# The last feed-forward layer's routing: experts ranked on the router's logits, softmax weights made on other engines, list keys in fewer steps

## The chip, the cores and the metric

One Trainium2 chip (trn2), one core. The metric is the device time of one execution of the whole program, in microseconds, as the median of several runs. The engines are named TensorE (PE, with its weight loads as PEld), VectorE (DVE), ScalarE (ACT), GpSimd (POOL) and SyncE (SP, which here only issues DMAs). L2147 is line 2147 of the kernel before.

## The reference

A network of four layers on x of 8 x 128 tokens with 256 features. Each layer adds an attention part and a feed-forward part, both on the layer-normalised x. Only the last feed-forward part is touched, a mixture of 64 experts with 8 for each token and room for 128 tokens in each expert:

```python
x = hidden_states.reshape(-1, H)                 # 1024 tokens, H = 256
logits = x @ router_weight.T                     # 64 experts
probs = softmax(logits, axis=-1)
topw, topi = top_k(probs, 8)
topw = topw / sum(topw, axis=-1, keepdims=True)
flat_e = topi.reshape(-1)
oh = one_hot(flat_e, E)
pos = take_along_axis(cumsum(oh, axis=0), flat_e[:, None], axis=1)[:, 0] - 1
xe = zeros((E, 128, H)).at[flat_e, pos].set(repeat(x, 8), mode='drop')
g, u = split(einsum('ech,ehf->ecf', xe, gate_up_proj), 2)   # 96 each
ye = einsum('eci,eih->ech', silu(g) * u, down_proj)
y_flat = where((pos < 128)[:, None], ye[flat_e, minimum(pos, 127)], 0)
y = sum(y_flat.reshape(-1, 8, H) * topw[..., None], axis=1)
```

A token whose place in an expert is 128 or later is dropped there.

## The kernel before, in words

The eight parts (four attentions, four feed-forwards) run one after the other, each a block with a program for every engine, ordered by semaphores. The last one is `moe_l3`. Tokens lie as 8 tiles (B) of 128 partitions, so that most of its routing steps are one instruction over 128 x (8 x 64) elements. `Chain` counts VectorE's steps: `link` issues a step and waits until it is done, `add` issues it alone, and `wait` waits for all steps added.

**Ahead of the experts**, in the order of the data:

- TensorE makes the logits in PSUM, `lg` (L2044).
- VectorE takes the row maximum (L2137) and subtracts it (L2138); ScalarE takes the exponential (L2112); VectorE sums (L2140), inverts (L2141) and multiplies (L2142). The probabilities are `ex`.
- VectorE takes the eight largest of each row (MAX8, L2144, 8 instructions), replaces them by -1 in a copy, `left` (MATCH_REPLACE with a value load, L2147, 8 pairs), and makes the 0/1 mask from it (L2149). `masked` is signalled.
- TensorE makes `pos` from the mask: how many earlier tokens chose the expert (L2050, 36 matmuls, `ranked`). Beside it VectorE makes the weights: sum of the eight best (L2150), inverse (L2151), product (L2152), product with the mask (L2155).
- VectorE counts along the row (scan, L2157), makes a number for each chosen slot, falling with the token (L2158), masks it (L2160), and sets it to zero where `pos` is 64 or more (L2162, the keys of list half one) and 128 or more (L2163); the difference is half two (L2164, `keyed`). L2165 zeroes the weights of dropped tokens (`weighed`), in `cw`.
- TensorE transposes the keys to expert x token (L2055, two groups of four). ScalarE copies group one (L2116) and VectorE group two (L2167) to SBUF.
- VectorE draws the 64 largest keys of each row, eight at a time: MAX8 (L2171) and MATCH_REPLACE (L2174) over 1024 elements, eight rounds. The list is turned (L2060) and made into slot numbers and token numbers (L2177 to L2180, `indexed`). Empty places point to a row of zeros.

**The token table** `xw` in HBM holds for each token its 256 features and 64 weights, and 128 zero rows. ScalarE's queue writes it with three DMAs: the features (L2108), the zero rows (L2110), and the weight columns when `weighed` (L2114). Each adds 16 to `table_in`.

**The experts' loop**: GpSimd gathers 128 rows for an expert with an indirect DMA (L2021), six experts ahead; the first needs `indexed` and all of `table_in`. TensorE turns them (L2068), multiplies (L2078), turns h (L2086), multiplies (L2093). ScalarE does Silu (L2124) and scales the result with the gathered weight (L2130). VectorE copies and multiplies (L2186, L2198, L2192). GpSimd scatters the 128 result rows to `rows` in HBM (L2026). SyncE prefetches the experts' weights in 16 loads of four experts (L1996), six of which start at once. At the end the eight rows of each token are read back and added on VectorE (L2210, L2211).

Of the kernel before, what the change touches and what calls it, by code (L numbers as in the profile page):

```python
# [12 lines left out]
ALU = mybir.AluOpType  # L13
ACT = mybir.ActivationFunctionType
AX = mybir.AxisListType.X

P = 128
D = 256
KD = D // P
B = 8  # L20
T = B * P
LN_EPS = 1e-5
HALF = 512
# [1908 lines left out]
def moe_l3(pg, pre, xw, rows):  # L1932

    nc, E, K, CAP, F = pg.nc, 64, 8, 128, 96
    GROUP, LOADS, AHEAD, NY = 4, 6, 6, 4
    ROW = D + E
    W = 2 * 2 * F + D
    names = ("const", "ones_in", "steps", "logits", "shifted", "exped", "masked", "ranked", "keyed", "weighed", "turned", "key_kept",
             "listed", "list_turned", "indexed", "table_in", "zero_in", "x_turned", "x_kept", "gu_done", "silued", "h_made", "h_turned",
             "h_kept", "y_done", "y_kept", "summed", "stored")  # L1940
    s = {m: pg.sem(f"l3m_{m}") for m in names}
# [4 lines left out]
    with ExitStack() as st:  # L1946
        def sb(m, shape, dt=F32):
            return st.enter_context(nc.sbuf_tensor(f"l3m_{m}", shape, dt))
        def wide_of(at, n):
            return pg.l2_wx[:].rearrange("p k n -> p (k n)")[:, at:at + n].rearrange("p (b e) -> p b e", b=B)  # L1950
        rw, = pre.tiles
        ex = wide_of(0, B * E)
# [3 lines left out]
        mt = wide_of(1536, B * E)  # L1956
        tmp = wide_of(2048, B * E)
        best = sb("best", [P, B, 8])
        small = sb("small", [P, 4, B])
# [47 lines left out]
        def _(pool):  # L2007
# [20 lines left out]

            pool.wait_ge(s["indexed"], 1)
# [77 lines left out]
        def _(act):  # L2107
# [4 lines left out]
            nc.scalar.activation(ex[:], ex[:], ACT.Exp).then_inc(s["exped"], 1)  # L2112
            act.wait_ge(s["weighed"], 1)
            act.dma_start(rows_of(xw)[:, :, D:ROW], cw[:]).then_inc(s["table_in"], 16)  # L2114
            act.wait_ge(s["turned"], 1)
            nc.scalar.activation(kb[:, 0, 0:HALF], key_ps[0][:], ACT.Copy).then_inc(s["key_kept"], 1)  # L2116
# [16 lines left out]
        def _(dve):  # L2133
# [3 lines left out]
            ch.link(v.tensor_reduce(small[:, 0, :], lg, AX, ALU.max))  # L2137
            v.tensor_tensor(ex[:], lg, small[:, 0, :].unsqueeze(2).to_broadcast(wide), ALU.subtract).then_inc(s["shifted"], 1)  # L2138
            dve.wait_ge(s["exped"], 1)
            ch.link(v.tensor_reduce(small[:, 1, :], ex[:], AX, ALU.add))  # L2140
            ch.link(v.reciprocal(small[:, 2, :], small[:, 1, :]))  # L2141
            ch.link(v.tensor_tensor(ex[:], ex[:], small[:, 2, :].unsqueeze(2).to_broadcast(wide), ALU.mult))  # L2142
            for t in range(B):
                ch.add(v.max(best[:, t, :], ex[:, t, :]))  # L2144
            ch.wait()
            for t in range(B):
                ch.add(v.match_replace(left[:, t, :], best[:, t, :], ex[:, t, :], -1.0))  # L2147
            ch.wait()
            v.tensor_scalar(mask[:], left[:], 0.0, None, ALU.is_lt).then_inc(s["masked"], 1)  # L2149
            ch.link(v.tensor_reduce(small[:, 0, :], best[:], AX, ALU.add))  # L2150
            ch.link(v.reciprocal(small[:, 3, :], small[:, 0, :]))  # L2151
            ch.link(v.tensor_tensor(ex[:], ex[:], small[:, 3, :].unsqueeze(2).to_broadcast(wide), ALU.mult))  # L2152
            dve.wait_ge(s["masked"], 1)
            dve.wait_ge(s["const"], 3)
            ch.add(v.tensor_tensor(ex[:], ex[:], mask[:], ALU.mult))  # L2155
            flat = mask[:].rearrange("p b e -> p (b e)")
            ch.link(v.tensor_tensor_scan(count[:], flat, flat, 0.0, ALU.add, ALU.max))  # L2157
            ch.link(v.scalar_tensor_tensor(out=mt[:], in0=count[:].rearrange("p (b e) -> p b e", b=B), scalar=-1.0,  # L2158
                                           in1=token[:].unsqueeze(2).to_broadcast(wide), op0=ALU.mult, op1=ALU.add))
            ch.link(v.tensor_tensor(mt[:], mt[:], mask[:], ALU.mult))  # L2160
            dve.wait_ge(s["ranked"], 1)
            ch.add(v.scalar_tensor_tensor(out=key[:, :, 0:E], in0=pos, scalar=float(CAP // 2), in1=mt[:], op0=ALU.is_lt, op1=ALU.mult))  # L2162
            ch.link(v.scalar_tensor_tensor(out=tmp[:], in0=pos, scalar=float(CAP), in1=mt[:], op0=ALU.is_lt, op1=ALU.mult))  # L2163
            v.tensor_tensor(key[:, :, E:2 * E], tmp[:], key[:, :, 0:E], ALU.subtract).then_inc(s["keyed"], 1)  # L2164
            v.scalar_tensor_tensor(out=cw[:], in0=pos, scalar=float(CAP), in1=ex[:], op0=ALU.is_lt, op1=ALU.mult).then_inc(s["weighed"], 1)  # L2165
# [201 lines left out]
```

## Time and profile before

| | us |
|---|---|
| median of 3 runs | 1994.09 |
| lowest and highest | 1990.58 to 1999.31 |
| the profiled execution | 1990.2 |
| its span | 1988.5 |
| TensorE busy (share of the span) | 1623.6 (82%) |
| VectorE busy | 1174.5 (59%) |
| ScalarE busy | 807.2 (41%) |
| GpSimd busy | 616.7 (31%) |

The span runs from the first to the last instruction of one profiled execution; the device time of that execution is a little longer. The granted TensorE clock is a share of its full speed of 2.4 GHz. A chain of work goes back from the last instruction, at each step to what released it. In a row of the timeline the brackets tell how long the engine sat idle before the instruction and what ended that.

### The profile page before, as it was taken

The page shows a single profiled execution, that of the slowest core. Times are in us where ns is not written, and L with a number is a line of the kernel's source. Part 1 is how long each engine was busy: PE and PEld are TensorE (multiplying, and loading weights), DVE is VectorE, ACT ScalarE, POOL GpSimd, SP SyncE. Part 2 cuts the span into 40 slices and gives each one's busy share as a digit, 9 for nine tenths or more (in the row PEclk, how much of TensorE's full clock was granted, in tenths as well). Part 3 has the DMA queues.
Part 4 walks back from the last instruction along what each step waited for, and adds up shares of the span by engine and source line. Part 5 has one row for each costly group of instructions (what it writes and reads, how often), then busy time and mean ns, then how long its engine had stood idle before and what let it go on. Part 6 is the DMA issues. An engine that isn't in the chain of part 4 may idle for free. (4 is left out here: it accounts for less than half of the span.)

```text
span 1988.5 us, 25186 instructions
## 1 busy us (share of the span) xinstructions
PE 1623.6 (82%) x8472; PEld 1004.2 (51%) x8472; DVE 1174.5 (59%) x2662; ACT 807.2 (41%) x1848; POOL 616.7 (31%) x979
## 2 busy tenths in 40 slices
PE   6688878999786899995388998998699989637772
PEld 5323234556454455553166666666555555435552
DVE  5799972223554642426789999999822255552325
ACT  3888773111322211112377777777621112312221
POOL 0022211000200197900455555655210000036662
PEclk9755558999687899997699999999899998767886
DMA  2288872110501213111100000000101100435635
GB/s 72 52 161 162 157 149 62 40 40 16 170 1 66 99 57 124 55 49 38 48 1 1 1 1 1 1 1 1 41 22 38 40 23 1 162 104 202 208 127 223
DMA packets 174224, 140.12 MB, mean 70 GB/s; under 512 B 141793, under 2 KB 154721, under 8 KB 170386
## 3 DMA queue, kind: packets, MB, share of 16 engines
q1 hardware_dynamic: 165314, 114.89, 20.6%
q0 software_dynamic: 6416, 22.03, 3.3%
q10 hardware_dynamic: 2368, 1.61, 0.3%
q8 instruction: 69, 1.13, 0.2%
q14 instruction: 57, 0.47, 0.1%
HBM read 85.43 MB, written 19.50 MB: 53 GB/s over the span
## 5 line engine op out<-in xcount | busy, mean ns | idle before, releaser
L1417 PE MATMUL l2x_pr<-l_w,l2x_xq 128*128 128x512 bf16 x576 | 142.4, 385 | 40.9 <-ACT credits L42 40.4
L350 PE MATMUL l1e_gu<-x_normT,l1e_w 128*128 128x512 f32 x384 | 170.8, 599 | 0.0
L1875 ACT ACTIVATE l0m_pf<-l0m_s,l0m_bias,l0x_sq 128x1024 int16<-128x1024 f32 x128 | 154.1, 1204 | 38.9 <-POOL l0m_bias L1807 38.9
L1901 DVE TENSOR_REDUCE l0m_mx<-l0m_s 128x1 f32<-128x1024 f32 x128 | 156.0, 1220 | 21.6 <-PE l0m_s L1817 20.1
L1817 PE MATMUL l0m_s<-l0x_kT,l0x_qT 48*128 48x512 bf16 x256 | 126.2, 620 | 35.8 <-ACT l0m_pf L1875 31.7
L350 PE MATMUL l0e_gu<-x_normT,l0e_w 128*128 128x512 f32 x272 | 121.5, 601 | 0.0
L1807 POOL TENSOR_SCALAR l0m_bias<-l0m_mx,l0x_nsq 128x1 f32<-128x1 f32 x128 | 46.7, 365 | 225.0 <-DVE l0m_mx L1901 223.6
L350 PEld LDWEIGHTS l1e_gu<-x_normT,l1e_w 128*128 128x128 f32 x384 | 73.8, 193 | 83.8 <-issue 82.7
L350 PE MATMUL l2e_gu<-x_normT,l2e_w 128*128 128x512 f32 x256 | 115.0, 604 | 0.0
L1546 DVE TENSOR_SCALAR l2x_raw<-l2x_raw,l2x_mv,l2x_rs 128x128 f32<-128x128 f32 x384 | 111.3, 352 | 3.5 <-POOL l2x_rs L1396 3.3
L1417 PEld LDWEIGHTS l2x_pr<-l_w,l2x_xq 128*128 128x128 bf16 x576 | 57.0, 99 | 97.3 <-ACT credits L42 40.8
L426 DVE TENSOR_TENSOR l1e_h<-l1e_sil,l1e_gu 128x512 f32<-128x512 f32 x40 | 27.5, 688 | 133.1 <-ACT l1e_sil L402 133.1
L1400 POOL TENSOR_TENSOR x_norm<-x_norm,l2x_rsm 128x512 f32<-128x512 f32 x64 | 74.9, 1171 | 97.2 <-DVE l2x_rsm L1552 97.2
L1536 DVE BATCH_NORM_STATS2 l2x_bn<-l2x_raw 128x6 f32<-128x128 f32 x384 | 82.5, 279 | 34.2 <-ACT l2x_raw L1485 34.1
L402 ACT ACTIVATE l1e_sil<-l1e_gu 128x512 f32<-128x512 f32 x48 | 28.6, 596 | 178.6 <-PE l1e_gu L350 178.6
L1437 PE MATMUL l2x_tr<-ident,l2x_raw 128*128 128x128 f32 x384 | 60.9, 281 | 44.7 <-DVE l2x_raw L1546 44.0
L1490 ACT ACTIVATE x_norm<-l2x_s,l2x_mx 128x128 f32<-128x128 f32 x256 | 90.3, 372 | 2.4 <-DVE l2x_mx L1541 2.4
L357 PE MATMUL l1e_y<-l1e_w,l1e_h 128*128 128x256 f32 x384 | 86.1, 379 | 0.0
L426 DVE TENSOR_TENSOR l0e_h<-l0e_sil,l0e_gu 128x512 f32<-128x512 f32 x28 | 19.3, 688 | 112.4 <-ACT l0e_sil L402 112.4
L1396 POOL TENSOR_TENSOR l2x_rs<-l2x_rs,l2x_half 128x8 f32<-128x8 f32 x48 | 82.7, 1723 | 3.8
L350 PEld LDWEIGHTS l0e_gu<-x_normT,l0e_w 128*128 128x128 f32 x272 | 52.4, 193 | 60.0 <-issue 59.3
L357 PEld LDWEIGHTS l1e_y<-l1e_w,l1e_h 128*128 128x128 f32 x384 | 73.0, 190 | 18.5 <-issue 9.6
(522 smaller groups left out, 3633.3 us busy)
## 6 DMA issues: line engine op xcount, KB each, us to landing
l3m_w<-in_l_moe SPq DMA_DIRECT2D x16, 1280.0 KB
l1e_w<-in_l_ffn SPq DMA_DIRECT2D x24, 384.0 KB, 3.1
l_rows<-zero_row SPq DMA_DIRECT2D x8, 1024.0 KB, 11.1
l_w<-l_rows SPq DMA_DIRECT2D x8, 1024.0 KB, 11.9
l0e_w<-in_l_ffn SPq DMA_DIRECT2D x17, 384.0 KB, 3.1
l2e_w<-in_l_ffn SPq DMA_DIRECT2D x16, 384.0 KB, 3.1
ctx_tok<-l_route SPq DMA_DIRECT2D x8, 512.0 KB
l2q_wps<-in_l_wp SPq DMA_DIRECT2D x16, 256.0 KB, 2.7
```

The source lines that it names most:

```text
L350: last = nc.tensor.matmul(gu[half][:, m, :], w[:, c % SW, (2 * k + m) * P:(2 * k + m + 1) * P], pg.xnT[:, k, cols(n)], start=(k == 0), sto ...
L357: last = nc.tensor.matmul(y[:, t, :], h[:, c % SH, t * P:(t + 1) * P], w[:, c % SW, WG:CHUNK], start=(c == 0 and t % 2 == 0), stop=False, ...
L1396: g.tensor_tensor(rs[:, 1, two, :], var, half[:, 0], ALU.pow).then_inc(s["rstd"], 1)
L1400: nc.gpsimd.tensor_tensor(p[:, a % 2], p[:, a % 2], rsm[:, a % 2].unsqueeze(2).to_broadcast([P, U, P]), ALU.mult).then_inc(s["p_normed"], 1)
L1417: last = nc.tensor.matmul(flat(pr[t % 2][:]), src[:, k, tokens], pg.l2_w3[:, part, k, at:at + W], start=(k == 0 and part == 0), stop=(k == ...
L1437: last = nc.tensor.transpose(tr[:, j, :], raw[:, u, j, :], pg.ident[:])
L1490: last = nc.scalar.activation(p[:, a % 2, j, :], s_ps[a % 2][:, j, :], ACT.Exp, bias=mx[:, a % 2, j:j + 1], accum_out=sm[:, a % 2, j:j + 1])
L1536: last = nc.vector.bn_stats(bn[:, t, j, :], raw[:, t, j, :])
L1546: last = nc.vector.tensor_scalar(raw[:, u, j, :], raw[:, u, j, :], mv[:, u, j, 0:1], rs[:, 1, u, j:j + 1], ALU.subtract, ALU.mult)
L1817: last = nc.tensor.matmul(s_ps[n % 3][:, g * HALF:(g + 1) * HALF], qT[:, h, b * P:(b + 1) * P], kT[:, h, g * HALF:(g + 1) * HALF], start=T ...
L1875: nc.scalar.activation(pf[:, n % 4, :], s_ps[n % 3][:], ACT.Exp, scale=sq[:, b, h:h + 1], bias=bias[:, n % 4:n % 4 + 1], accum_out=sm[:, b ...
L1901: nc.vector.tensor_reduce(mx[:, n % 4:n % 4 + 1], s_ps[n % 3][:], AX, ALU.max).then_inc(s["maxed"], 1)
```

## The change

The rank is taken on the logits, which softmax leaves in the same order. VectorE draws the eight largest logits (`best`), makes the negated maximum from the first, replaces the eight in a copy and makes the mask. ScalarE makes, beside it, the exponentials of the eight best with their sum (8 instructions with an accumulator output) and, once the mask is done, the exponentials of all 64 logits with the negated maximum as bias (8 instructions). VectorE inverts the sums of eight after the keys, and GpSimd multiplies, which gives `cw` with no mask: weights of experts that a token did not choose are never gathered. ScalarE copies the first half of the turned keys before it waits for `weighed` and issues the weight columns' DMA. The keys of half one are no longer cut at place 64 nor those of half two at place 128, since the lists hold 64 each and take the earliest tokens first; half two keeps the places from 64 on.

```diff
@@ -1934,8 +1934,9 @@
+    GONE = -3.0e38
@@ -1953,10 +1954,10 @@
         mask = sb("mask", [P, B, E], BF16)
-        mt = wide_of(1536, B * E)
         tmp = wide_of(2048, B * E)
         best = sb("best", [P, B, 8])
-        small = sb("small", [P, 4, B])
+        top = sb("top", [P, B, 8])
+        small = sb("small", [P, 3, B])
@@ -2026,6 +2027,9 @@
                 g.indirect_dma_start(out=rows, out_offset=bass.IndirectOffsetOnAxis(ap=slot[:, e:e + 1], axis=0),
                                      in_=ye[:, e % NY, :], in_offset=None).then_inc(put[e % NY], 16)
 
+            pool.wait_ge(s["exped"], B)
+            pool.wait_ge(s["top_inverse"], 1)
+            g.tensor_tensor(cw[:], ex[:], small[:, 2, :].unsqueeze(2).to_broadcast([P, B, E]), ALU.mult).then_inc(s["weighed"], 1)
             pool.wait_ge(s["indexed"], 1)
             pool.wait_ge(s["table_in"], 48)
             for e in range(AHEAD):
@@ -2109,11 +2113,16 @@
             act.wait_ge(s["zero_in"], 1)
             act.dma_start(xw[T:T + P, :], zero[:]).then_inc(s["table_in"], 16)
             act.wait_ge(s["shifted"], 1)
-            nc.scalar.activation(ex[:], ex[:], ACT.Exp).then_inc(s["exped"], 1)
+            for n in range(B):
+                nc.scalar.activation(top[:, n, :], best[:, n, :], ACT.Exp, bias=small[:, 0, n:n + 1], accum_out=small[:, 1, n:n + 1])\
+                    .then_inc(s["summed_top"], 1)
+            act.wait_ge(s["masked"], 1)
+            for n in range(B):
+                nc.scalar.activation(ex[:, n, :], lg[:, n, :], ACT.Exp, bias=small[:, 0, n:n + 1]).then_inc(s["exped"], 1)
+            act.wait_ge(s["turned"], 1)
+            nc.scalar.activation(kb[:, 0, 0:HALF], key_ps[0][:], ACT.Copy).then_inc(s["key_kept"], 1)
             act.wait_ge(s["weighed"], 1)
             act.dma_start(rows_of(xw)[:, :, D:ROW], cw[:]).then_inc(s["table_in"], 16)
-            act.wait_ge(s["turned"], 1)
-            nc.scalar.activation(kb[:, 0, 0:HALF], key_ps[0][:], ACT.Copy).then_inc(s["key_kept"], 1)
 
             for i in range(E + 2):
                 if 1 <= i <= E:
@@ -2134,35 +2143,26 @@
             v, ch = nc.vector, Chain(dve, s["steps"])
             wide = [P, B, E]
             dve.wait_ge(s["logits"], 1)
-            ch.link(v.tensor_reduce(small[:, 0, :], lg, AX, ALU.max))
-            v.tensor_tensor(ex[:], lg, small[:, 0, :].unsqueeze(2).to_broadcast(wide), ALU.subtract).then_inc(s["shifted"], 1)
-            dve.wait_ge(s["exped"], 1)
-            ch.link(v.tensor_reduce(small[:, 1, :], ex[:], AX, ALU.add))
-            ch.link(v.reciprocal(small[:, 2, :], small[:, 1, :]))
-            ch.link(v.tensor_tensor(ex[:], ex[:], small[:, 2, :].unsqueeze(2).to_broadcast(wide), ALU.mult))
-            for t in range(B):
-                ch.add(v.max(best[:, t, :], ex[:, t, :]))
+            for n in range(B):
+                ch.add(v.max(best[:, n, :], lg[:, n, :]))
             ch.wait()
-            for t in range(B):
-                ch.add(v.match_replace(left[:, t, :], best[:, t, :], ex[:, t, :], -1.0))
+            v.tensor_scalar(small[:, 0, :], best[:, :, 0], -1.0, None, ALU.mult).then_inc(s["shifted"], 1)
+            for n in range(B):
+                ch.add(v.match_replace(left[:, n, :], best[:, n, :], lg[:, n, :], GONE))
             ch.wait()
-            v.tensor_scalar(mask[:], left[:], 0.0, None, ALU.is_lt).then_inc(s["masked"], 1)
-            ch.link(v.tensor_reduce(small[:, 0, :], best[:], AX, ALU.add))
-            ch.link(v.reciprocal(small[:, 3, :], small[:, 0, :]))
-            ch.link(v.tensor_tensor(ex[:], ex[:], small[:, 3, :].unsqueeze(2).to_broadcast(wide), ALU.mult))
+            v.tensor_scalar(mask[:], left[:], GONE, None, ALU.is_le).then_inc(s["masked"], 1)
             dve.wait_ge(s["masked"], 1)
             dve.wait_ge(s["const"], 3)
-            ch.add(v.tensor_tensor(ex[:], ex[:], mask[:], ALU.mult))
             flat = mask[:].rearrange("p b e -> p (b e)")
             ch.link(v.tensor_tensor_scan(count[:], flat, flat, 0.0, ALU.add, ALU.max))
-            ch.link(v.scalar_tensor_tensor(out=mt[:], in0=count[:].rearrange("p (b e) -> p b e", b=B), scalar=-1.0,
+            ch.link(v.scalar_tensor_tensor(out=tmp[:], in0=count[:].rearrange("p (b e) -> p b e", b=B), scalar=-1.0,
                                            in1=token[:].unsqueeze(2).to_broadcast(wide), op0=ALU.mult, op1=ALU.add))
-            ch.link(v.tensor_tensor(mt[:], mt[:], mask[:], ALU.mult))
+            ch.link(v.tensor_tensor(key[:, :, 0:E], tmp[:], mask[:], ALU.mult))
             dve.wait_ge(s["ranked"], 1)
-            ch.add(v.scalar_tensor_tensor(out=key[:, :, 0:E], in0=pos, scalar=float(CAP // 2), in1=mt[:], op0=ALU.is_lt, op1=ALU.mult))
-            ch.link(v.scalar_tensor_tensor(out=tmp[:], in0=pos, scalar=float(CAP), in1=mt[:], op0=ALU.is_lt, op1=ALU.mult))
-            v.tensor_tensor(key[:, :, E:2 * E], tmp[:], key[:, :, 0:E], ALU.subtract).then_inc(s["keyed"], 1)
-            v.scalar_tensor_tensor(out=cw[:], in0=pos, scalar=float(CAP), in1=ex[:], op0=ALU.is_lt, op1=ALU.mult).then_inc(s["weighed"], 1)
+            v.scalar_tensor_tensor(out=key[:, :, E:2 * E], in0=pos, scalar=float(CAP // 2), in1=key[:, :, 0:E], op0=ALU.is_ge, op1=ALU.mult)\
+                .then_inc(s["keyed"], 1)
+            dve.wait_ge(s["summed_top"], B)
+            v.reciprocal(small[:, 2, :], small[:, 1, :]).then_inc(s["top_inverse"], 1)
             dve.wait_ge(s["turned"], 2)
             v.tensor_copy(kb[:, 0, HALF:T], key_ps[1][:]).then_inc(s["key_kept"], 1)
             dve.wait_ge(s["key_kept"], 2)
```

## Rows read from the trace of the kernel before

**Rows 1.** Stretches: ranking and keys, lists, experts' loop.
```profile
core 0: us, PE busy (x) PEld busy (x) DVE busy (x) ACT busy (x) POOL busy (x), PEclk, DMA share, GB/s
1726.60:1742.10 15.50, 4.00 (x44) 3.52 (x44) 12.97 (x41) 1.39 (x3) 0.00 (x0) 0.50 1.01 416
1742.10:1763.80 21.70, 0.52 (x5) 0.29 (x4) 20.36 (x27) 1.12 (x1) 0.00 (x0) 0.50 0.10 28
1763.80:1956.70 192.90, 139.63 (x576) 106.55 (x576) 57.18 (x192) 45.79 (x128) 124.83 (x128) 0.78 0.50 165
```

**Rows 2.** Chain that ended last, in order of time: start us, us, what.
```profile
1726.61 0.70 DVE l3m_small L2137
...
1728.06 0.64 ACT l_wx L2112
...
1730.41 1.13 DVE l3m_best L2144 x8
...
1731.56 1.66 DVE l_wx L2147 x9
1733.21 0.02 issue
1733.23 0.43 DVE l3m_mask L2149
...
1739.43 0.70 DVE l_wx L2164
```

**Rows 3.** Timeline: start us, us, engine, line; idle before and its releaser last.
```profile
1735.40 1.22 DVE L2157 TENSOR_TENSOR_SCAN l_wx<-l3m_mask 128x512 f32<-128x512 bf16 x1
...
1735.64 0.24 PE L2050 MATMUL l3m_ps<-l3m_mask,l3m_before 128*128 128x64 bf16 x1
...
1740.75 0.38 ACTq L2114 DMA_DIRECT2D l_xw<-l_wx  x1
1741.33 0.60 ACT L2116 ACTIVATE l_w<-l3m_ps 128x512 f32<-128x512 f32 x1 [12.64 <-PE l3m_ps L2055]
...
1742.18 0.69 DVE L2167 COPY l_w<-l3m_ps 128x512 f32<-128x512 f32 x1 [1.46 <-PE l3m_ps L2055]
...
1764.04 1.15 POOL L2021 DMA_INDIRECT l3m_xg<-l_xw,l3m_idx  x1 [43.48 <-DVE l3m_idx L2180]
```

**Rows 4.** Groups of instructions, shapes apart: busy us, mean ns | idle before, releasers.
```profile
L2164 DVE TENSOR_TENSOR l_wx<-l_wx 128x512 f32<-128x512 f32 x1 | 0.7, 693 | 0.0
...
L2137 DVE TENSOR_REDUCE l3m_small<-l3m_ps 128x8 f32<-128x512 f32 x1 | 0.7, 692 | 7.4 <-PE l3m_ps L2044 7.4
...
L2140 DVE TENSOR_REDUCE l3m_small<-l_wx 128x8 f32<-128x512 f32 x1 | 0.7, 686 | 0.7 <-ACT l_wx L2112 0.7
...
L2141 DVE RECIPROCAL l3m_small<-l3m_small 128x8 f32<-128x8 f32 x1 | 0.2, 203 | 0.0
...
L2124 ACT ACTIVATE l3m_sil<-l3m_ps 128x96 f32<-128x96 f32 x64 | 16.1, 251 | 132.0 <-PE l3m_ps L2078 71.0 <-remote 44.8 <-issue 16.0
```

**Rows 5.** Timeline of ScalarE in an earlier layer, exponentials with an accumulator.
```profile
1002.48 0.37 ACT L1490 ACTIVATE x_norm<-l2x_s,l2x_mx 128x128 f32<-128x128 f32 x1 [0.95 <-DVE l2x_mx L1541]
1002.75 0.19 ACT L1490 ACTIVATION_READ_ACCUMULATOR x_norm<-l2x_s,l2x_mx 128x1 f32 x1
1002.84 0.36 ACT L1490 ACTIVATE x_norm<-l2x_s,l2x_mx 128x128 f32<-128x128 f32 x1
```

**Rows 6.** One line's instructions on GpSimd: duration ns min/median/max, first and last start.
```profile
L1400 POOL TENSOR_TENSOR x_norm<-x_norm,l2x_rsm x64: 1034/1129/1378, 1002.6 to 1421.5; 128x512 f32<-128x512 f32 x64
```

**Rows 7.** DMA issues of the last layer: KB each, median us to landing.
```profile
l_xw<-l_wx ACTq DMA_DIRECT2D x1, 256.0 KB, 5.3
l_xw<-l3m_zero ACTq DMA_DIRECT2D x1, 160.0 KB, 24.0
```

**Rows 8.** Two stretches of the experts' loop, columns as in rows 1.
```profile
1800.00:1810.00 10.00, 9.18 (x33) 7.87 (x34) 3.21 (x11) 2.07 (x6) 5.89 (x6) 0.57 0.43 139
1870.00:1880.00 10.00, 4.95 (x25) 3.38 (x25) 2.22 (x8) 1.49 (x5) 7.13 (x8) 1.00 0.67 234
```

More of the change, by code:

```diff
@@ L1936, in moe_l3 @@
     ROW = D + E
+    GONE = -3.0e38
     W = 2 * 2 * F + D
-    names = ("const", "ones_in", "steps", "logits", "shifted", "exped", "masked", "ranked", "keyed", "weighed", "turned", "key_kept",
+    names = ("const", "ones_in", "steps", "logits", "shifted", "summed_top", "top_inverse", "exped", "masked", "ranked", "keyed", "weighed", "turned", "key_kept",
              "listed", "list_turned", "indexed", "table_in", "zero_in", "x_turned", "x_kept", "gu_done", "silued", "h_made", "h_turned",
```

## The prediction, made blind

> **What bounds the kernel now.** The profiled execution took 1990.2 us, with a span of 1988.5 us and 1.7 us around it. The median of the three timed runs is 1994.09 us, 3.9 us above the profiled one. The runs themselves lie between 1990.58 and 1999.31 us. I make the sum on the span and then take it off the median.
>
> I read three views, in this order. First, the stretches of the last layer [rows 1]. The ranking and key stretch lasts 15.5 us. VectorE is busy for 12.97 of it and TensorE for 4.00. Behind it come 21.7 us in which VectorE alone makes the lists (20.36 busy), and then 192.9 us of expert loop, where no engine is full: TensorE 139.6 busy, GpSimd 124.8. So a step saved on VectorE ahead of the loop moves everything behind it. Second, the chain of work that ended last, in order of time [rows 2]. From 1726.61 to 1740.13 it runs through every VectorE step of the ranking, with one 0.64 us ScalarE step between. Nothing else is on it: the whole softmax stands in line ahead of the ranking. Third, the single instructions with their starts [rows 3], for what the other engines have ready, and when.
>
> **The path to the keys, before.** It starts at 1726.61 and ends with the subtraction at 1739.43 + 0.70 = 1740.13, so 13.52 us [rows 2].
>
> **The path to the keys, after.** A link, a step that waits for the one before it, costs 0.02 us, as at 1733.21 [rows 2].
> - Eight MAX8 on the logits 1.13, link 0.02, negation of 128x8 taken at 0.20 as the reciprocal of the same shape [rows 4], eight MATCH_REPLACE with their value loads 1.66, link 0.02, mask 0.43 [rows 2]. The sum is 3.46 us, so the mask is done at 1730.07 instead of 1733.66.
> - Wait on the mask, taken a little over a link, 0.03, scan 1.22 at its full length [rows 3], link 0.02, two 512-element steps with a link each, 2 x 0.71, and one last 512-element step 0.69 [rows 4]. The sum is 3.38 us, so the keys are done at 1733.45.
> - Sum 6.84 against 13.52: **6.68 us less**, of which 3.59 ahead of the mask (two reductions, subtraction, exponential, reciprocal, multiplication, less the new negation) and 3.09 behind it (second normalisation, mask product, one of the two position tests, the subtraction).
>
> **Logits read where they lie.** MAX8 and MATCH_REPLACE now read PSUM, which no row shows for them. The nearest pair is a reduction of 512 elements, 692 ns from PSUM and 686 ns from SBUF [rows 4]. I take 6 ns for each of 16 instructions, 0.1 us, which I leave in the range. The row's difference, nothing against 0.1, gives both ends. The Trainium skill (VectorE: DVE Perf Modes, "The TRN2 errata") gives VectorE 120 fixed cycles for a PSUM source against 58 for an SBUF one, at 0.96 GHz. By the page, as an estimate, the 16 instructions would cost 1.0 us more, and the gain would be 5.7. The reduction's two rows speak against it.
>
> **The position counts.** The chain must not wait for TensorE. Its last count matmul ended at 1735.64 + 0.24 = 1735.88, 2.22 us after the mask [rows 3]. After the change that is 1732.29, and VectorE asks for it at 1732.76. The cover is 0.47 us. If the matmuls take longer than that, the excess is lost one for one. Their clock cannot fall: it is at its lower level, 0.50 or 1.2 GHz, through both stretches, with 4.00 of 15.5 us busy [rows 1].
>
> **ScalarE's new work.** It may start at 1728.0. Eight exponentials with an accumulator: the nearest rows are pairs of an ACTIVATE of 128x128 and an accumulator read, which start 0.36 us apart [rows 5]. So 2.9 us is the upper end, and 2.1 the lower, with 120 elements less at 0.84 ns, which the 512-wide copy's 0.60 us and the 96-wide Silu's 0.25 us give (0.35 us for 416 elements) [rows 3, 4]. Eight exponentials of 128x64: between 0.25 (the 96-wide Silu, no bias operand) [rows 4] and 0.36 each [rows 5], 2.0 to 2.9 us. ScalarE is free between 1732.1 and 1733.8. What hides it is the position part of the chain. ScalarE's next duty is the copy of the first half of the transposed keys. It began 1.20 us after the keys [rows 2, 3], now 1734.65, so 0.85 to 2.55 us of cover are left. A further 0.9 us stands behind it, because VectorE's own half ended later (1742.87 against 1741.93) [rows 3]. If that cover goes, VectorE's first list round waits for the copy.
>
> **GpSimd's multiplication.** It waits for those exponentials and for the reciprocal behind the keys (1733.45 + 0.20). Two-input products of 128x512 on GpSimd take 1034 to 1378 ns [rows 6], so it ends between 1734.7 and 1735.2. Queued behind it on GpSimd are only the gathers, which wait for the indices until 1757 anyway. It reads SBUF while VectorE waits for the transposes. VectorE loses a product of 512 elements (0.69) and gains the reciprocal (0.20), both behind the keys and ahead of a wait for TensorE that lasted 1.46 us [rows 3], so they cost nothing.
>
> **The weight column's DMA.** It is the same DMA, but now queued behind ScalarE's copy: issue at about 1735.3 instead of 1740.75 [rows 3]. It moves no other step back, since the Silu table load behind it is needed only in the loop. Its landing took 5.3 us, that of the zero block, issued into the weight prefetch, 24.0 us [rows 7]. That gives 1740.6 to 1759.3. The gathers want it at 1757.4. I take the lower end plus some wait, about 1746: the DMA share falls from 1.01 to 0.10 at 1742.1 [rows 1], so nothing is left to queue behind. The upper end would cost 1.9 us.
>
> **The lists and the loop.** List rounds, transposes, indices, gathers and the experts' loop are the same instructions, moved up by 6.7 us. The first gather should start at 1764.04 - 6.68 = 1757.36. By the span: 1988.5 - 6.7 = 1981.8, by the profiled execution 1990.2 - 6.7 = 1983.5, by the median **1994.1 - 6.7 = 1987.4 us**.
>
> **The rivals.**
> - *ScalarE becomes the bound (chance 0.10).* If ScalarE ended 3.8 us later than its upper bound (0.85 + 0.9 of cover, then 2 us on the path), or the weight column landed at its upper end (1.9 us), some 2 us come back: 1989.4 us. For it: 24 ScalarE instructions stand where one did. Against it: 0.85 us of cover at the upper bounds.
> - *The loop runs better in its new place (chance 0.15).* The loop is 29 times as long as the gain. GpSimd is busy for 124.8 of 192.9 us, and in two stretches of ten microseconds the granted clock is 0.57 and 1.00 [rows 8], means over its two levels (0.50 is 1.2 GHz, 1.00 is 2.4 GHz). If a sixth of the 30 us that TensorE's half-clock time costs went away (139.6 us at 0.78 is 109 at full clock), that is 5 us: 1982.4 us. Against it: nothing inside the loop is changed, so it is chance.
> - *The loop falls badly (chance 0.05), slower than before.* The place is the experts' loop, and the mechanism the granted clock. 139.6 us of TensorE work at a mean of 0.78 [rows 1] become 146.3 at 0.744, which eats the whole gain, and 156.3 at 0.697, which is the point where the kernel is 0.5% slower, if all of it lies on the path. At 0.73 the cost is 9.6 us and the time 1997.0. For it: the timed runs of one kernel already span 8.7 us. Against it: a mean over 193 us has to move. The Trainium skill (TensorE: Matmul & The Clock Gate, Part 1) says that the number of slow matmuls at the start of the same kernel changes from run to run; one trace cannot show that here. By that rule the loop's time could drift either way, and no step of the change steers it.
>
> **How the numbers follow.** The forecast, 6.7 us less, has 0.70. A measurement of this kernel can tell some 0.5% from no change, which is 10 us; the forecast is 0.34%, so it counts as within 0.5%. Faster by more than that needs a time under 1984.1: the second rival, and a little of the forecast's scatter, 0.19 together. Slower needs over 2004: part of the third rival, 0.03. The rest, 0.78, is within 0.5%. The range: downwards the scatter of the median (1994.09 - 1990.58 = 3.5) and half of the second rival's extra, which gives 1981; upwards 5.2 for the scatter (1999.31 - 1994.09) and 2.4 for the first rival, 1995.
>
> **What would show it.** Right: MAX8 at the start of the chain, mask about 3.5 us after the logits, last key step about 6.8 us after them; ScalarE done with its sixteen exponentials before its copy of the keys; the first gather near 1757.4; a loop of 193 us, give or take 5. Wrong: idle time of the first list round or of VectorE's key copy released by ScalarE, idle time of the last key step released by the counts, MAX8 of 64 elements clearly over 0.14 us apart, the first gather released by the weight column's DMA, or a loop whose length moved by more than the gain.

## The result, and the profile after

| | before | after |
|---|---|---|
| median of 20 runs, us | 1995.14 | 1988.17 |
| lowest and highest | 1990.58 to 2001.98 | 1983.2 to 1994.02 |
| profiled execution, span | 1990.2, 1988.5 | 1987.75, 1986.0 |

The ratio of after to before is 0.9961, 95% interval 0.9951 to 0.9971: 7.8 us less, between 5.8 and 9.8. The medians lie 7.0 us apart. The interval lies clear of 1, so the kernel is faster, but by less than the 0.5% that the forecast set as its line; it counts as within 0.5%, as forecast.

The stretches of the changed kernel's last layer, cut at the same events as before (busy us and count of each engine, granted clock, DMA share, GB/s). They answer to [rows 1]:

```profile
core 0: us, PE busy (x) PEld busy (x) DVE busy (x) ACT busy (x) POOL busy (x), PEclk, DMA share, GB/s
1730.38:1739.22 8.84, 4.01 (x44) 3.52 (x44) 6.75 (x31) 4.74 (x26) 1.05 (x1) 0.50 1.04 429
1739.22:1760.90 21.68, 0.52 (x5) 0.29 (x4) 20.36 (x27) 1.12 (x1) 0.00 (x0) 0.50 0.41 150
1760.90:1954.32 193.42, 135.88 (x576) 103.83 (x576) 56.98 (x192) 45.22 (x128) 124.84 (x128) 0.81 0.49 165
```

From the logits to the start of VectorE's copy of the turned keys are 8.84 us where it was 15.5. The lists (21.68 against 21.70) and the loop (193.4 against 192.9) keep their lengths. ScalarE is busy for 4.74 us instead of 1.39, GpSimd for 1.05 instead of nothing.

The chain that ended last (start us, us, what), which answers to [rows 2]:

```profile
1730.39 1.16 DVE l3m_best L2147 x8
...
1731.58 0.17 DVE l3m_small L2149
1731.75 1.60 DVE l_wx L2151 x8
...
1733.37 0.44 DVE l3m_mask L2153
...
1733.83 1.24 DVE l_wx L2157
...
1736.55 0.70 DVE l_wx L2162
...
1737.29 1.99 PE l3m_ps L2059 x8
...
1739.30 0.70 DVE l_w L2167
```

It starts at 1730.39 and the last key step ends at 1737.25: **6.86 us** against 13.52. No ScalarE and no GpSimd piece stands in it. Ahead of the mask's end lie 3.42 us (the prediction had 3.46), behind it 3.44 (3.38).

Single instructions of the other engines, from the timeline (idle time and its releaser in brackets), which answer to [rows 3]:

```profile
1734.08 1.70 ACT L2121 ACTIVATE l_wx<-l3m_ps,l3m_small 128x64 f32<-128x64 f32 x8
...
1735.78 0.24 PE L2054 MATMUL l3m_ps<-l3m_mask,l3m_before 128*128 128x64 bf16 x1
...
1737.50 1.05 POOL L2032 TENSOR_TENSOR l_wx<-l_wx,l3m_small 128x512 f32<-128x512 f32 x1 [13.15 <-DVE l3m_small L2165]
1738.45 0.60 ACT L2123 ACTIVATE l_w<-l3m_ps 128x512 f32<-128x512 f32 x1 [2.68 <-PE l3m_ps L2059]
1738.58 0.38 ACTq L2125 DMA_DIRECT2D l_xw<-l_wx  x1
...
1761.16 1.15 POOL L2022 DMA_INDIRECT l3m_xg<-l_xw,l3m_idx  x1 [22.61 <-DVE l3m_idx L2180]
```

The last count matmul ends at 1736.02, and the key step that needs it starts at 1736.55. ScalarE's sixteen exponentials end at 1735.78, and it sits idle for 2.68 us before its copy of the keys. The first gather is released by the indices.

All profiled executions can be laid side by side at the end of the logits. The table holds milestones read from their timelines, in us, those marked + counted from that end; "loop" runs from the first gather's start to the last scatter's end. The kernels of one letter B, C or D ran on one chip, with before beside them; A are the two of the result.

| kernel | logits end at | first transpose | first list round | first gather | loop | group |
|---|---|---|---|---|---|---|
| before | 1726.57 | +13.60 | +16.34 | +37.47 | 193.6 | A |
| after | 1730.36 | +6.93 | +9.67 | +30.80 | 194.1 | A |
| a_rank_only | 1726.45 | +8.26 | +10.99 | +32.12 | 179.5 | B |
| b_keys_only | 1729.66 | +12.27 | +15.00 | +36.13 | 175.1 | B |
| e_dve9 | 1728.09 | +13.45 | +16.18 | +37.31 | 177.6 | B |
| e_dve28 | 1728.17 | +27.28 | +30.01 | +51.14 | 178.1 | B |
| c_pool8 | 1728.61 | +6.94 | +9.67 | +30.80 | 180.5 | C |
| c_pool24 | 1731.00 | +6.94 | +9.67 | +38.59 | 177.3 | C |
| d_act_order | 1728.18 | +6.93 | +9.66 | +30.79 | 180.6 | C |
| before_again | 1728.56 | +13.59 | +16.33 | +37.46 | 194.3 | D |
| after_again | 1728.42 | +6.93 | +9.66 | +30.78 | 194.1 | D |
| f_act16 | 1727.60 | +6.93 | +11.48 | +32.60 | 193.8 | D |
| h_halves | 1733.71 | +4.54 | +7.27 | +28.40 | 194.4 | D |

In the two profiled executions of the first two lines the first gather is 6.67 us closer to the logits. The spans differ by only 2.5 us, since the parts ahead of the last one, where nothing was changed, happened to take 3.79 us longer (1730.36 - 1726.57) and the loop 0.5 us, less 0.1 behind it: 3.79 - 6.67 + 0.5 - 0.1 = -2.5. In the second pair of the same two kernels, before_again and after_again, the logits end within 0.14 us of each other and the loops are 0.2 us apart, and there the spans differ by 7.1 us (1991.2 and 1984.1).

### The profile page after: what moved, and what is told of

Its sections match the earlier page's. It is cut to its first block and busy times, and to the rows that moved or that the text cites. A ratio compares the mean times of both kernels' runs of the same rounds, so it can differ in the third digit from the quotient of the medians.

```text
span 1986.0 us, 25201 instructions
## 1 busy us (share of the span) xinstructions
PE 1622.9 (82%) x8472; PEld 1004.9 (51%) x8472; DVE 1170.6 (59%) x2652; ACT 809.9 (41%) x1871; POOL 616.7 (31%) x980
## 3 DMA queue, kind: packets, MB, share of 16 engines
q8 instruction: 69, 1.13, 0.2%
## 5 line engine op out<-in xcount | busy, mean ns | idle before, releaser
L1901 DVE TENSOR_REDUCE l0m_mx<-l0m_s 128x1 f32<-128x1024 f32 x128 | 155.8, 1219 | 21.8 <-PE l0m_s L1817 20.3
L402 ACT ACTIVATE l1e_sil<-l1e_gu 128x512 f32<-128x512 f32 x48 | 28.6, 596 | 179.4 <-PE l1e_gu L350 179.4
L426 DVE TENSOR_TENSOR l0e_h<-l0e_sil,l0e_gu 128x512 f32<-128x512 f32 x28 | 19.3, 688 | 110.7 <-ACT l0e_sil L402 110.7
L357 PEld LDWEIGHTS l1e_y<-l1e_w,l1e_h 128*128 128x128 f32 x384 | 72.9, 190 | 19.4 <-issue 9.1
```

The costliest lines, as they stand in the source:

```text
L357: last = nc.tensor.matmul(y[:, t, :], h[:, c % SH, t * P:(t + 1) * P], w[:, c % SW, WG:CHUNK], start=(c == 0 and t % 2 == 0), stop=False, ...
L1901: nc.vector.tensor_reduce(mx[:, n % 4:n % 4 + 1], s_ps[n % 3][:], AX, ALU.max).then_inc(s["maxed"], 1)
```

## The experiments

**Half of the change each.** First the ranking on the logits with the weights beside it, and the keys as before:

```diff
 after, with the keys of before:
...
-            v.scalar_tensor_tensor(out=key[:, :, E:2 * E], in0=pos, scalar=float(CAP // 2), in1=key[:, :, 0:E], op0=ALU.is_ge, op1=ALU.mult)\
-                .then_inc(s["keyed"], 1)
+            ch.add(v.scalar_tensor_tensor(out=key[:, :, 0:E], in0=pos, scalar=float(CAP // 2), in1=mt[:], op0=ALU.is_lt, op1=ALU.mult))
+            ch.link(v.scalar_tensor_tensor(out=tmp[:], in0=pos, scalar=float(CAP), in1=mt[:], op0=ALU.is_lt, op1=ALU.mult))
+            v.tensor_tensor(key[:, :, E:2 * E], tmp[:], key[:, :, 0:E], ALU.subtract).then_inc(s["keyed"], 1)
```

> The half of the change ahead of the mask: ranking on the logits and weights on ScalarE and GpSimd, but the keys made from the position counts in three steps, as before. Theory 1 (the gain is the VectorE steps taken off the chain, one for one): from the last logits to the finished keys 13.52 in the profile of before, 6.86 in that of after; here 6.86 plus two 512-element steps behind the counts (0.61 + 0.72, or about 1.35) = 8.2 us, so the first gather 5.3 us earlier behind the logits than before, ratio to before 0.9973. Theory 2 (the gain sits mainly in the fewer key steps, or comes from the loop's place): under 3 us here, ratio above 0.9985 or no order between the two halves.

Timeline of VectorE and TensorE in this kernel:

```profile
1726.49 1.15 DVE L2148 MAX8 l3m_best<-l3m_ps 128x8 f32<-128x64 f32 x8 [7.42 <-PE l3m_ps L2049]
...
1732.64 0.69 DVE L2163 SCALAR_TENSOR_TENSOR l_wx<-l3m_ps,l_wx 128x512 f32<-128x512 f32 x1
...
1733.96 0.69 DVE L2165 TENSOR_TENSOR l_wx<-l_wx 128x512 f32<-128x512 f32 x1
...
1734.71 1.97 PE L2060 MATMUL l3m_ps<-ident,l_wx 128*128 128x128 f32 x8 [2.59 <-DVE l_wx L2165]
```

From 1726.49 to the first transpose at 1734.71 are 8.22 us, with three key steps instead of one (6.90 in the changed kernel, 1730.39 to 1737.29). The first gather comes at +32.12, 5.35 us ahead of before's. The time was 1969.99 us against 1978.47 for before on that chip, ratio 0.9958 (0.9944 to 0.9972). The trace hits the expectation to 0.1 us. The time gained 8.5 us, more than the 5.35 us, and its interval ends at 5.5, so by time this half gained slightly more than its path explains; where the rest comes from is open.

Then the other half, the key steps alone on the kernel before (the same diff the other way round):

> The other half alone: softmax, second normalisation and mask product stay ahead, as before; only the keys are made in fewer steps. Theory 1: 13.52 - 1.35 = 12.2 us from the logits to the keys, first gather 1.35 us earlier, ratio to before 0.9993, not to be told from no change by time, only in the trace. Theory 2: most of the 6.7 us here, ratio about 0.9966.

```profile
1729.70 0.69 DVE L2137 TENSOR_REDUCE l3m_small<-l3m_ps 128x8 f32<-128x512 f32 x1 [7.42 <-PE l3m_ps L2044]
...
1741.18 0.69 DVE L2162 SCALAR_TENSOR_TENSOR l_wx<-l3m_ps,l_wx 128x512 f32<-128x512 f32 x1
...
1741.93 1.97 PE L2055 MATMUL l3m_ps<-ident,l_wx 128*128 128x128 f32 x8 [2.96 <-DVE l_wx L2162]
```

From the maximum at 1729.70 to the first transpose at 1741.93 are 12.23 us (13.56 before, 1726.61 to 1740.17), and the first gather comes at +36.13, 1.34 us earlier. The time was 1973.93 us, ratio 0.9984 (0.9968 to 0.9999), which holds the expected 0.9993. On the path the halves add up: 5.35 + 1.34 = 6.69, against 6.67 for the whole change. Theory 2 falls on the path: four fifths of the gain lie in the first half. By time b_keys_only gained 3.2 us (0.2 to 6.3), an interval that holds its 1.34 us of path.

**The chain lengthened again.** The changed kernel, with needless products ahead of the last key step:

```diff
             ch.link(v.tensor_tensor(key[:, :, 0:E], tmp[:], mask[:], ALU.mult))
+            for _i in range(9):      # 28 in the other kernel
+                ch.link(v.tensor_tensor(wide_of(1536, B * E)[:], tmp[:], mask[:], ALU.mult))
```

> The changed kernel with nine needless linked VectorE products of 512 elements (0.72 us each, 6.5 us) put ahead of the last key step. Everything else of the change stays: weights on ScalarE and GpSimd, fewer ScalarE waits. Theory 1: the gain is only a shorter chain, so this is the time of before within 0.1% (ratio 1.000, 6.86 + 6.5 = 13.4 us from logits to keys). Theory 2 (something of the gain lies off the VectorE chain, in the loop, the weight column or the engines' load): clearly below 1.000, 0.998 or less.

The first gather stood at +37.31, before's at +37.47. The time was 1976.63 us against 1978.47, ratio 0.9988 (0.9976 to 1.0001). With the chain back at its old length the gain is gone to within the interval, although ScalarE and GpSimd still do the weights. That is 0.12% under before, a little outside the 0.1% of theory 1 and short of the 0.998 of theory 2. The interval reaches up to 4.7 us of gain, so by time a small part off the chain is not ruled out; the trace shows none ahead of the first gather.

> The same with 28 such products, 20.2 us. Theory 1: one for one, 20.2 us over the changed kernel, 13.5 us over before, ratio 1.0068. Rival (the loop or the table swallows part of a delay, or answers it with more): the excess over the changed kernel outside 18 to 22 us.

The 28 products as one group (busy us, mean ns | idle before them):

```profile
L2162 DVE TENSOR_TENSOR l_wx<-l_wx,l3m_mask 128x512 f32<-128x512 f32 x28 | 19.4, 693 | 1.0
```

The first gather stood at +51.14, 20.34 us behind after's. The time was 1992.77 us, 14.3 over before and ratio 1.0069 (1.0053 to 1.0085), where 13.7 (51.14 - 37.47) or 1.0069 was due. So time added on this stretch of VectorE's chain counts one for one, in the trace and, within the interval of 10.5 to 16.8 us, in the time.

**The weight path's cover.** More multiplications on GpSimd ahead of the real one, into a spare region, each waiting for the one before:

```diff
+            extra = Chain(pool, pg.sem("l3m_extra"))
+            for _i in range(8):      # 24 in the other kernel
+                extra.link(g.tensor_tensor(wide_of(1536, B * E)[:], ex[:], small[:, 2, :].unsqueeze(2).to_broadcast([P, B, E]), ALU.mult))
             g.tensor_tensor(cw[:], ex[:], small[:, 2, :].unsqueeze(2).to_broadcast([P, B, E]), ALU.mult).then_inc(s["weighed"], 1)
```

> The changed kernel with eight more multiplications on GpSimd ahead of the real one, about 1.1 us each with their links, so the weights are ready 9 us later (about 1747.5 on the clock of the changed kernel's profile), and the weight column's DMA is issued then. It landed 11.9 us after its issue there, 5.3 us in the profile of before. Theory (the weight path has cover until the gathers): landing at 1753 to 1759 against a first gather at 1761.2, so no time is lost, ratio as for the changed kernel, 0.996. Rival (the weight column holds the first gather already): the 9 us show, ratio 1.0005.

GpSimd's timeline:

```profile
1735.76 8.89 POOL L2034 TENSOR_TENSOR l_wx<-l_wx,l3m_small 128x512 f32<-128x512 f32 x8 [13.16 <-DVE l3m_small L2168]
1744.72 1.04 POOL L2035 TENSOR_TENSOR l_wx<-l_wx,l3m_small 128x512 f32<-128x512 f32 x1
1759.41 1.15 POOL L2022 DMA_INDIRECT l3m_xg<-l_xw,l3m_idx  x1 [13.65 <-DVE l3m_idx L2183]
```

And the DMA of the weight column in this kernel (KB, us to landing):

```profile
l_xw<-l_wx ACTq DMA_DIRECT2D x1, 256.0 KB, 2.8
```

The eight took 8.89 us, and the first gather kept its place to the hundredth, +30.80, released by the indices. The weight column's DMA was issued at 1745.79, 17.2 us behind the logits, and landed 2.8 us later. On the clock of the changed kernel's profile that is 1750.3, ahead of the 1753 to 1759 that the expectation had. The time was 1972.2 us against 1976.48, ratio 0.9982 (0.9973 to 0.9992). That is less than the 0.996 expected and the 0.9966 that 6.67 us of path make (1 - 6.67 / 1976); d_act_order on the same chip has 0.9971 (0.9961 to 0.9981). The ratio lies between the two forecasts and its interval holds neither, so the trace decides here and not the time. The intervals of c_pool8 and d_act_order overlap, nothing ahead of the loop accounts for a difference in the trace, and the loops of the two are equal (180.5 and 180.6 us). Why the median of c_pool8 lies so near before's stays open.

> The same with 24 more, about 27 us: weights ready at 1765.5, past the indices at 1760.9. The queues are empty by then, so 5.3 us for the DMA give 1771, and a first gather about 10 us later than in the changed kernel, released by the DMA or the table: ratio about 1.001. If it lands after 11.9 us as in the changed kernel's profile, 16 us later, ratio 1.004. Rival (a hidden path stays hidden): 0.996.

```profile
1738.14 26.87 POOL L2034 TENSOR_TENSOR l_wx<-l_wx,l3m_small 128x512 f32<-128x512 f32 x24 [13.15 <-DVE l3m_small L2168]
1765.09 1.04 POOL L2035 TENSOR_TENSOR l_wx<-l_wx,l3m_small 128x512 f32<-128x512 f32 x1
1769.59 1.15 POOL L2022 DMA_INDIRECT l3m_xg<-l_xw,l3m_idx  x1 [3.46 <-DMA l_xw<-l_wx]
```

And the DMA of the weight column in this kernel (KB, us to landing):

```profile
l_xw<-l_wx ACTq DMA_DIRECT2D x1, 256.0 KB, 2.6
```

Now the DMA releases the first gather, at +38.59, 7.79 us later than in the changed kernel. The expectation had some 10: the landing took 2.6 us, not 5.3. The time was 1976.87 us, ratio 1.0001 (0.9992 to 1.0011); by the path the kernel should be 1.12 us behind before, 1.0006, which the interval holds. So the weight path is hidden up to a point and counts beyond it. The two runs bracket that point: a landing 10.8 us ahead of the first gather (c_pool8) costs nothing on the path, and one some 7 us past that place (37.8 us behind the logits, c_pool24) costs 7.8. That fits the point where the prediction has it, at the indices.

**ScalarE's order of before**, with the wait for the weights and their DMA ahead of the copy of the keys:

```diff
+            act.wait_ge(s["weighed"], 1)
+            act.dma_start(rows_of(xw)[:, :, D:ROW], cw[:]).then_inc(s["table_in"], 16)
             act.wait_ge(s["turned"], 1)
             nc.scalar.activation(kb[:, 0, 0:HALF], key_ps[0][:], ACT.Copy).then_inc(s["key_kept"], 1)
-            act.wait_ge(s["weighed"], 1)
-            act.dma_start(rows_of(xw)[:, :, D:ROW], cw[:]).then_inc(s["table_in"], 16)
```

> The changed kernel with ScalarE's order of before: it waits for the weights and issues their DMA first, and copies the first half of the turned keys behind that. In the changed kernel's profile GpSimd's product ended at 1738.55 and the copy began at 1738.45 and ended at 1739.05, 0.94 ahead of VectorE's own half. Here it should begin some 0.1 to 0.5 us later, within that cover: first list round as in the changed kernel, 9.64 us behind the last logits, ratio 0.996. Rival (the moved copy is what makes the gain): 0.5 to 1 us later lists, or more.

```profile
1736.82 0.60 ACT L2125 ACTIVATE l_w<-l3m_ps 128x512 f32<-128x512 f32 x1 [3.23 <-POOL l_wx L2032]
1737.12 0.69 DVE L2167 COPY l_w<-l3m_ps 128x512 f32<-128x512 f32 x1 [1.95 <-PE l3m_ps L2059]
```

The copy now waits for GpSimd's product and comes 8.64 us behind the logits instead of 8.09, and still ends (1737.42) ahead of VectorE's half (1737.81). The first list round stands at +9.66. The time was 1970.6 us, ratio 0.9971 (0.9961 to 0.9981). The moved copy buys 0.55 us of cover that nothing used.

**ScalarE loaded until it shows.** Sixteen more exponentials ahead of the copy of the keys, a chain of their own:

```diff
+            extra = Chain(act, pg.sem("l3m_extra"))
+            for _i in range(16):
+                extra.link(nc.scalar.activation(wide_of(1536, B * E)[:, _i % B, :], lg[:, _i % B, :], ACT.Exp, bias=small[:, 0, _i % B:_i % B + 1]))
             act.wait_ge(s["turned"], 1)
```

> The changed kernel with 16 more exponentials of 128x64 on ScalarE ahead of the copy of the keys, each waiting for the one before, about 0.35 us each, 5.5 us. ScalarE was idle for 2.68 us before that copy, and the copy ended 0.94 us ahead of VectorE's half. Theory (cover as predicted, then one for one): the first list round 5.5 - 2.7 - 0.9 = 1.9 us later, 11.6 us behind the last logits instead of 9.67. Rival (no cover): 5.5 us later. Rival (hidden anyway): no shift.

```profile
1732.88 5.53 ACT L2124 ACTIVATE l_wx<-l3m_ps,l3m_small 128x64 f32<-128x64 f32 x16
...
1738.44 0.60 ACT L2126 ACTIVATE l_w<-l3m_ps 128x512 f32<-128x512 f32 x1
...
1739.08 1.23 DVE L2174 MAX8 l3m_lst<-l_w 128x8 f32<-128x1024 f32 x1 [1.85 <-ACT l_w L2126]
```

The sixteen lasted 5.53 us, and the first list round waits 1.85 us for ScalarE's copy. It stands at +11.48, 1.81 us later than in the changed kernel, where 1.9 was expected. So a late ScalarE does hold the chain, but only after 3.7 us more of its work. The kernel has a single timed run (1986.53 us), so only its trace is read.

**The same two kernels on one chip.** The loops of groups B and C looked longer where they started early, so both kernels ran once more beside each other.

> The changed kernel once more, for its loop and its time on the chip of this call. Theory 1: 6.7 us less than before outside the loop, a loop of the same length as before's on this chip within 3 us, ratio 0.995 to 0.998. Rival (the loop is longer where it starts early, by some 3 us, as the loops of 180.5 and 180.6 us against 175.1 to 178.1 us in the runs with a later start suggest): ratio 0.998 or above, and a loop of 180 us or more against 178 or less.

> The kernel before once more as a kernel of its own, for its loop on the same chip and for the scatter of two samples of one kernel. Theory 1: ratio within 0.999 to 1.001, first gather 37.4 us behind the logits, loop as in after_again within 3 us. Rival (late start, short loop): a loop at least 3 us shorter than after_again's.

after_again: 1986.5 us against 1995.54, ratio 0.9964 (0.9948 to 0.9981), loop 194.1 us. before_again: 1992.37 us, ratio 0.9992 (0.9976 to 1.0007), loop 194.3 us. The two medians lie 5.9 us apart, where the path has 6.7. The rival falls on this chip: a start 6.8 us earlier left the loop within 0.2 us. In groups B and C before's own loop was not profiled, so there it stays open. There the three loops that start 30.8 to 32.1 us behind the logits took 179.5 to 180.6 us, the four that start at 36.1 or later 175.1 to 178.1. The medians do not settle it: a_rank_only and b_keys_only lie 3.9 us apart with 4.0 us of path between them, as if the loops were equal, while c_pool8 and c_pool24 lie 4.7 apart with 7.8 of path.

**A further version.** The logits lie in two banks, and VectorE ranks tiles 0 to 3 while TensorE still multiplies for tiles 4 to 7:

```diff
+        lg_of = [gu_ps[0][:].rearrange(...), h_ps[1][:].rearrange(...)]
...
+            for a in range(2):
+                lo, hi = a * h2, (a + 1) * h2
+                dve.wait_ge(s["logits"], a + 1)
...
+                v.tensor_scalar(mask[:, lo:hi, :], left[:, lo:hi, :], GONE, None, ALU.is_le).then_inc(s["masked"], 1)
+                v.tensor_scalar(small[:, 0, lo:hi], best[:, lo:hi, 0], -1.0, None, ALU.mult).then_inc(s["shifted"], 1)
...
+                start = 0.0 if a == 0 else count[:, lo * E - 1:lo * E]
+                ch.link(v.tensor_tensor_scan(count[:, cols], flat[:, cols], flat[:, cols], start, ALU.add, ALU.max))
```

> A further version: the logits of tiles 0 to 3 and 4 to 7 lie in two PSUM banks, and VectorE ranks, counts and numbers the first four tiles while TensorE makes the logits of the others; ScalarE starts its sums of eight in two parts as well. Behind the last logits are left four MAX8 0.58, four MATCH_REPLACE 0.80, mask of 256 elements 0.29, negation 0.12, scan 0.69, two steps of 256 elements 0.88, the last key step 0.70 and the links: 4.15 us against 6.86, if the counts are ready; TensorE's 26 later count matmuls may hold the last step by up to 0.45. Theory (the chain ahead of the lists counts one for one): first gather 28.1 to 28.6 us behind the last logits instead of 30.8, 2.2 to 2.7 us less than the changed kernel, ratio to before about 0.9953. Rival (TensorE's logits or the shared PSUM slow the first half's work, or the loop takes it back): first gather above 30.

```profile
1730.33 0.63 DVE L2157 MAX8 l3m_best<-l3m_ps 128x8 f32<-128x64 f32 x4 [4.01 <-PE l3m_ps L2050]
...
1733.43 0.42 DVE L2172 TENSOR_TENSOR l_wx<-l_wx,l3m_mask 128x256 f32<-128x256 f32 x1
...
1737.04 0.43 DVE L2172 TENSOR_TENSOR l_wx<-l_wx,l3m_mask 128x256 f32<-128x256 f32 x1
...
1737.14 0.24 PE L2058 MATMUL l3m_ps<-l3m_mask,l3m_before 128*128 128x64 bf16 x1
1737.50 0.69 DVE L2174 SCALAR_TENSOR_TENSOR l_wx<-l3m_ps,l_wx 128x512 f32<-128x512 f32 x1
...
1738.25 1.97 PE L2063 MATMUL l3m_ps<-ident,l_wx 128*128 128x128 f32 x8 [0.86 <-DVE l_wx L2174]
```

VectorE starts at 1730.33, 3.4 us before the logits end, and is through with the first four tiles 0.14 us after the last logits (1733.85 against 1733.71). The last count matmul ends at 1737.38, and the last key step starts at 1737.50 behind VectorE's own step, so the counts do not hold it. The transposes start at +4.54 instead of +6.93, the first gather at +28.40 instead of +30.80. The time was 1984.6 us against 1995.54, ratio 0.9946 (0.9927 to 0.9965). The 2.4 us over the changed kernel are shown on the path; by time its interval overlaps after_again's, and the first gather lies within the 28.1 to 28.6 us expected.

## Why the prediction was right

It gave 1987.4 us and the median is 1988.17. The gain is what it was right about: 6.7 us forecast, 6.67 found on the path, by the mechanism that it names. That the level came so near is partly luck, since it starts from a median of three runs, 1994.09, and the median of 20 is 1995.14; from that the same gain gives 1988.4. In its range, the upper end adds 2.4 us for a rival that it prices at 2.0; nothing hangs on that. Step by step:

- **The path to the keys**: 6.84 predicted, 6.86 found, 13.52 before. Shown by the chain and, half by half, by a_rank_only and b_keys_only. The negation and the MATCH_REPLACE steps behind it took 0.17 + 1.60 = 1.77 on the chain instead of 1.86, since the one starts before the other has ended; MAX8 took 1.16 instead of 1.13, and the steps behind the mask 3.44 instead of 3.38. The sum came closer than its terms: 0.04 too much ahead of the mask and 0.06 too little behind it nearly cancel.
- **Logits read from PSUM.** Eight MAX8 cost 0.03 us more. Single instructions, after first and before second (busy us, mean ns):

```profile
L2117 ACT ACTIVATE l3m_top<-l3m_best,l3m_small 128x8 f32<-128x8 f32 x8 | 2.3, 288 | 6.2 <-DVE l3m_small L2149 6.2
...
L2151 DVE MATCH_REPLACE8 l_wx<-l3m_best,l3m_ps 128x64 f32<-128x64 f32 x8 | 1.6, 212 | 0.0
...
L2117 ACT ACTIVATION_READ_ACCUMULATOR l3m_top<-l3m_best,l3m_small 128x1 f32 x8 | 1.5, 187 | 0.0
...
L2147 DVE MAX8 l3m_best<-l3m_ps 128x8 f32<-128x64 f32 x8 | 1.2, 217 | 7.4 <-PE l3m_ps L2048 7.4
```

```profile
L2147 DVE MATCH_REPLACE8 l_wx<-l3m_best,l_wx 128x64 f32<-128x64 f32 x8 | 1.6, 208 | 0.0
...
L2144 DVE MAX8 l3m_best<-l_wx 128x8 f32<-128x64 f32 x8 | 1.1, 211 | 0.0
```

MAX8 takes 217 ns from PSUM and 211 from SBUF, MATCH_REPLACE 212 and 208: 6 and 4 ns, as the reduction of [rows 4] said. As an estimate from the 62 cycles between the two figures of the Trainium skill (VectorE: DVE Perf Modes, "The TRN2 errata") it would have been 65 each. The measurement decides: no such step shows here.
- **The counts**: cover 0.47 predicted, 0.53 found (1736.55 - 1736.02).
- **ScalarE**: the eight sums start 0.28 us apart, 2.3 us in all, near the lower end; the eight exponentials took 1.70, under the 2.0 that the prediction had as the lower end. That end took the duration of one instruction, 0.25 us, as its step. Here one lasts 306 ns, but eight take 1.70 us in all, so they overlap and start some 0.20 us apart. So the cover was 2.68 us, above the 0.85 to 2.55 predicted. The rival in which ScalarE becomes the bound needed 3.6 us more work; f_act16 shows that it then comes one for one.
- **GpSimd**: 1051 ns within 1034 to 1378, ended 1738.55, which is 8.19 behind the logits; predicted 1734.7 to 1735.2 against logits at 1726.57, so 8.1 to 8.6.
- **The weight column**: issued 8.22 us behind the logits (predicted 8.7), since the DMA issue stands 0.13 us behind the start of ScalarE's copy (1738.58 and 1738.45) and not behind its end; it landed after 11.9 us:

```profile
l_xw<-l_wx ACTq DMA_DIRECT2D x1, 256.0 KB, 11.9
```

That is 20.1 us behind the logits, where about 19.4 was predicted, and 10.7 before the gather. c_pool24 shows that it would count if it were later than the indices. The guess came near, but not for the reason given. The prediction lets the DMA share fall at 1742.1, "so nothing is left to queue behind", and 1742.1 is only where [rows 1] cuts its stretches. Cut finer, the DMA engines are full until 1744, 17.4 us behind the logits, in the kernel before (first two lines), and until 1748, 17.6 us behind them, in the changed one (last two; columns as in [rows 1]):

```profile
1742.00:1744.00 2.00, 0.14 (x1) 0.00 (x0) 1.79 (x2) 1.22 (x1) 0.00 (x0) 0.50 1.03 300
1744.00:1746.00 2.00, 0.00 (x0) 0.00 (x0) 1.93 (x4) 0.00 (x0) 0.00 (x0) 0.50 0.06 17
...
1746.00:1748.00 2.00, 0.00 (x0) 0.00 (x0) 1.93 (x4) 0.00 (x0) 0.00 (x0) 0.50 1.03 299
1748.00:1750.00 2.00, 0.00 (x0) 0.00 (x0) 1.97 (x3) 0.00 (x0) 0.00 (x0) 0.50 0.07 20
```

So an earlier issue only waits longer. It did no harm here, because the gathers want the column 10.7 us later still.
- **Lists and loop**: moved up whole. e_dve9 and e_dve28 show one for one, back to the old length and 13.7 us beyond it. The loop kept its length, so neither the better nor the worse loop came about: the granted clock of the loop went from 0.78 to 0.81 and its length from 192.9 to 193.4, so the clock was not what sets it. Group D says the same: granted clocks of 0.77 (f_act16) and 0.82 (after_again), and loops of 193.8 and 194.1 us.

What the path explains is 6.67 us. The measured 7.8 (5.8 to 9.8) agrees with it.

One thing in the description of the change has to be set right: weights of experts that a token did not choose are gathered. A gather fetches whole rows of the table, with all 64 weights; the loop reads only the column of its own expert (`D + e`), so the others are never used, and that is why the mask can go.

## What to carry to other kernels

Where a chain of one engine stands ahead of everything that follows, its steps can be priced from the rows of their like and taken off one for one; here the sum came within 0.02 us on a path of 6.9, with two errors of about 0.05 that cancelled. Put beside the chain what only the weights of the results need. Here that is the softmax: it keeps the order of the logits, so the ranking does not have to wait for it. Then work out for each engine that takes it over when its next duty on the chain falls due. If a step waits for a whole batch of tiles, look whether half of them are ready earlier: that gave another 2.4 us on the path.

## What the runs showed of the hardware beyond that

- The same 256 KB write took 5.3 us to land when issued 14 us behind the logits (before), 11.9 when issued 8 us behind them (after), and 2.6 when issued 35 us behind them (c_pool24). Issued 6 us earlier, it landed no earlier: 19.5 us behind the logits before (14.18 + 5.3), 20.1 after (8.22 + 11.9). It is so in all eleven profiled executions that issued it between 6.2 (h_halves, landing after 13.9) and 17.2 us (c_pool8, after 2.8) behind the logits: it landed 19.3 to 20.3 us behind them. The DMA share is about 1 until 17.4 to 17.6 us behind the logits in before and after. Whether the column waits there for the weight prefetch from SyncE's queue, or for the features and zero rows that stand ahead of it in its own, no run separates.
- The experts' loop took 193.6 to 194.4 us in six profiled executions of groups A and D and 175.1 to 180.6 in seven of groups B and C, whatever the kernel, and the median of before went from 1995 to 1978 and 1976 us with it. The loop's granted clock was 0.77 to 0.82 in the first and 0.84 to 0.87 in the second. Only a comparison on one chip can tell a change of 7 us. What differs between the chips was not tried.
- GpSimd products of two inputs, 1.11 to 1.12 us apart, ran beside VectorE's list rounds without slowing them: MAX8 and MATCH_REPLACE of 1024 elements kept their 1.23 and 1.21 us in c_pool8 and c_pool24. One step behind the lists was held. In c_pool24, whose products still ran then, the step that makes the slot numbers took 0.56 us instead of the 0.20 of c_pool8:

```profile
1761.09 0.56 DVE L2182 TENSOR_SCALAR l3m_slot<-l3m_idxf 128x64 int32<-128x64 f32 x1
...
1758.70 0.20 DVE L2182 TENSOR_SCALAR l3m_slot<-l3m_idxf 128x64 int32<-128x64 f32 x1
```

A GpSimd product ran from 1760.55 to 1761.59 there, and the step ended at 1761.65, just behind it. The indices came 0.36 us later by it, which cost nothing, since the weights came later still. It is one instruction in one trace. In the changed kernel GpSimd's product (1737.50 to 1738.55) falls where VectorE waits for the transposes.
